# A graph network kernel on one core: the memset behind each gather of source rows is dropped

## What is computed

```python
h = relu(layernorm(x))
# layer 1: attention over the edges, 4 heads of 16
ZU = einsum('nd,kdr->knr', h, U)
zs, zd = ZU[:, src, :], ZU[:, dst, :]
logits = (zs * zd).sum(-1) / 4
alpha = softmax of logits over the edges of one dst
agg = segment_sum(alpha[..., None] * zs, dst)
x = x + relu(gradient step of h and agg with U, Dmat)
h = relu(layernorm(x))
# layer 2: message passing and a GRU cell
red = segment_sum(h[src] + relvectors[edge_type], dst)
x = x + gru(red, h)
```

## Time and profile before

| | us |
|---|---|
| median of 3 runs | 1061.5 (1060.14 to 1062.06) |
| span of the profiled execution | 1059.6 |
| gathers of source rows, first to last start | 46.87 to 722.93 |
| first and last weighing (L1083) start | 121.0 and 733.6 |
| second layer, about | 747 to 1059 |

### The profile page before, as it was taken

How to read it: one execution, slowest core, us unless ns; L and a number is a source line. 1 busy time by engine, 2 the same in 40 slices (tenths; PEclk the granted TensorE clock), 3 DMA queues, 4 the chain that set the end, 5 groups by cost and what they waited for, 6 DMA issues and landing times.

```text
span 1059.6 us, 14242 instructions
## 1 busy us (share of the span) xinstructions
PE 862.7 (81%) x4828; PEld 640.4 (60%) x4828; DVE 631.8 (60%) x1285; ACT 421.5 (40%) x804; POOL 647.8 (61%) x969
## 2 busy tenths in 40 slices
PE   6943688787788878787887786676999999999996
PEld 6741676565566656565665564464676676677773
DVE  5340577787888867777777764453243343388853
ACT  5423216555555555555565543341211111124441
POOL 4698888888888888888888888883001001000000
PEclk9996557787777777777787787787999999999998
DMA  9361334445455544554454553323344434421111
GB/s 196 77 156 36 74 78 120 119 119 125 116 128 130 132 123 112 129 123 125 119 129 111 120 124 89 88 51 84 95 126 141 124 116 137 124 87 49 50 51 34
DMA packets 54646, 112.99 MB, mean 107 GB/s; under 512 B 15435, under 2 KB 32968, under 8 KB 51443
## 3 DMA queue, kind: packets, MB, share of 16 engines
q1 hardware_dynamic: 34632, 81.38, 24.1%
q0 software_dynamic: 18880, 30.57, 17.5%
q10 hardware_dynamic: 1056, 0.07, 0.1%
HBM read 80.99 MB, written 30.86 MB: 106 GB/s over the span
## 4 chain that ended last, share of the span: by engine, by line
POOL 57%; PE 31%; issue 7%; DVE 2%; DMA 1%; SPq 1%; ACT 1%; POOLq 0%; DVEq 0%; ACTq 0%
POOL shared L724 28%; POOL cnt_rows L729 15%; POOL zs_third L724 13%; PE bank L1948 13%; PE bank L1947 6%; PE bank L1974 5%; PE bank L1975 2%; PE bank L1925 1%; PE bank L1875 1%; PE bank L1707 1%; PE bank L1971 1%; PE bank L1966 1%; DMA xs<-in_x 0%; DVE bst L885 0%; SPq L471 0%
## 5 line engine op out<-in xcount | busy, mean ns | idle before, releaser
L724 POOL DMA_INDIRECT shared<-zu_table,src_col x306 | 300.0, 980 | 51.6 <-issue 48.7
L729 POOL MEMSET cnt_rows<- 54x300 f32 x450 | 165.5, 368 | 0.3
L724 POOL DMA_INDIRECT zs_third<-zu_table,src_col x144 | 140.8, 978 | 23.0 <-issue 23.0
L999 DVE TENSOR_TENSOR setup<-iota_b,bank 128x500 bf16<-128x500 bf16 (+1 forms) x252 | 140.0, 609 | 1.1 <-PE bank L1911 0.5
L1570 ACT ACTIVATE setup<-bank 125x500 bf16<-125x500 f32 (+1 forms) x126 | 81.2, 681 | 106.5 <-PE bank L1911 70.7
L1804 PEld LDWEIGHTS bank<-zus,shared 125*128 125x128 f32 x900 | 114.0, 209 | 15.5 <-issue 14.9
L1804 PE MATMUL bank<-zus,shared 125*128 125x64 f32 x900 | 115.6, 292 | 7.8 <-ACT shared L1515 5.9
L1829 PE MATMUL bank<-layer,oh 128*125 128x84 f32 x900 | 110.1, 284 | 0.0
L1829 PEld LDWEIGHTS bank<-layer,oh 128*125 128x125 f32 x900 | 107.7, 200 | 0.1
L1911 PE MATMUL bank<-setup 128*125 128x125 bf16 x450 | 58.3, 279 | 52.0 <-DVE setup L999 42.9
L1911 PEld LDWEIGHTS bank<-setup 128*125 128x125 bf16 x450 | 48.4, 184 | 78.2 <-DVE setup L999 70.7
(11 more groups left out here) (235 smaller groups left out, 1775.8 us busy)
## 6 DMA issues: line engine op xcount, KB each, us to landing
shared<-in_edges SPq DMA_DIRECT2D x25, 1125.0 KB
counts_table<-setup SPq DMA_DIRECT2D x18, 683.6 KB
own_table<-own_out SPq DMA_DIRECT2D x25, 375.0 KB
shared<-own_table SPq DMA_DIRECT2D x25, 375.0 KB
zus<-counts_table POOLq DMA_DIRECT2D x9, 683.6 KB, 5.2
shared<-counts_table POOLq DMA_DIRECT2D x9, 683.6 KB, 5.0
shared<-zu_table,src_col POOLq DMA_INDIRECT x306
h_table<-h2s SPq DMA_DIRECT2D x25, 125.0 KB
```

The source lines that it names most:

```text
L724: nc.gpsimd.indirect_dma_start(out=zs[t % 3][:, j * KR:(j + 1) * KR], out_offset=None, in_=zu_table, in_offset=bass.IndirectOffsetOnAxis(a ...
L729: nc.gpsimd.memset(idle, 0.0).then_inc(idle_set, 1)
L999: nc.vector.tensor_tensor(chunk[n % 2][:, 0:(b - a) * W].rearrange("p (g w) -> p g w", w=W), io, ps(3, 128, at + a, at + b).unsqueeze(2).b ...
```

## The change

The memset and the wait ahead of it are taken out of the loop over columns, and with them the region, the semaphore and its first increment. Nothing else is touched.

```diff
-        idle = cnt_rows[0:3 * C, N - 300:N]
...
-        idle_set = sem("idle_set")
...
                             in_offset=bass.IndirectOffsetOnAxis(ap=src_col[:, t, j:j + 1], axis=0),
                         ).then_inc(g_zs[t % 3][c], 16)
-                        pool.wait_ge(idle_set, t * C + j + 1)
-                        nc.gpsimd.memset(idle, 0.0).then_inc(idle_set, 1)
 
             def windowed():
-                pool.sem_inc(idle_set, 1)
                 pool.wait_ge(st_zu, 16 * 2 * 5)
                 each_window(source_rows)
```

## The result

The median is 1387.6 us (4 runs, 1379.5 to 1389.4) against 1061.5 us for the kernel before in the same comparison. The ratio is 1.305, with a 95% interval of 1.301 to 1.309. The kernel became 30% slower. The forecast, 1075.5 us with a range of 1014 to 1084, was far off in size, and its mechanism isn't what happened.

A forecast was written before the change was run, and what follows sets the result against it. GpSimd's gather stream was taken to bound the first layer. The profiled span of 1059.6 us, plus 450 x (1.509 - 1.478) = 14 us for a later last gather, plus 1.9 carried over, gave 1075.5 us; range 1014 to 1084.

The forecast's parts named there:

- What bounds the kernel: First layer: its end hangs on GpSimd's last gather; GpSimd's chain ends last for 57% of the span.
- The distance between gathers: GpSimd, first layer: start of one gather to the next, predicted to go from 1.478 to 1.509 us.
- the second way: GpSimd's gather distance taken from setup gathers without a memset, record 1.20 plus gap 0.30: 1.509 us, 0.031 longer.
- the first way: GpSimd's gather distance as today's 0.953 us record plus the setup's 0.30 gap: 1.257 us, 0.221 less than now.
- what would make me wrong: Closing caveat: that the extra 0.25 us in the fifteen setup gathers' records come from their extra descriptors.
- packets are 2.5 times as many and the record is only a quarter longer: Setup gathers against the loop's: reason given for doubting that extra descriptors make their records longer.
- The whole shift lands: First layer: all 14 us by which the last gather starts later reach the end, since VectorE waits for gathers.
- rival *Faster: First layer: the memset is 0.22 us of pure delay per gather; end 46 us sooner, around 1015.5 us; chance 31%.
- rival *No change: GpSimd: memset lies wholly beside something done anyway between gathers; distance stays 1.478 us, time 1061.5 us; chance 13%.
- The worth of a shorter distance: Gather stream: each 0.01 us below a distance of 1.478 gives 4.5 us, up to a distance of about 1.38.

The follow-up runs named there:

- e15: Kernel before with the memset behind each gather 1x300 instead of 54x300: 1044.6 us, ratio 0.985.
- e18: Kernel before with the memset behind each gather 1x150 instead of 54x300: 995.5 us, ratio 0.939.
- e1: Kernel before with the memset behind each gather 1x1 instead of 54x300, wait and increment kept: 1400.7 us, ratio 1.319.
- e4: Kernel before with the 54x300 memset and its wait only behind each sixth gather: 1381.3 us, ratio 1.301.
- e11: Kernel before with a second memset of 54x30, with its own wait, added behind the 54x300 one: 1138.4 us, ratio 1.072.
- e9: Kernel before without the memset, each gather waiting until the one before it has landed: 1847.0 us, ratio 1.739.
- e5: Kernel before with the memset behind each gather 54x150 instead of 54x300: 1261.3 us, ratio 1.188.
- e12: Kernel before with the memset 54x150 instead of 54x300 from window 20 on only: 1107.7 us, ratio 1.043.
- e6: Kernel before with the memset behind each gather 54x230 instead of 54x300: 1140.4 us, ratio 1.066 from its two shortest runs.
- e13: Changed kernel with each gather fetching rows for 64 partitions instead of 128, buffers cleared once ahead: 992.2 us, ratio 0.935 against before.
- e14: Changed kernel with each gathered row 16 floats instead of 64, buffers cleared once ahead: 993.3 us, ratio 0.937 against before.
- e8: Kernel before with twelve 1x1 memsets behind each gather in place of the 54x300 one: 1089.8 us, ratio 1.025.

## Why the prediction was wrong

**What bounds the kernel** was read rightly. The first layer hung on the gather stream, and e15 to e18, each against before on its own chip, return nearly what the last gather gains: 16.7 us sooner gave 15.3 us (e15), 67.8 gave 64.8 (e18). The second layer kept its length: from the last weighing to the end 325.1 us, and 326.0 before.

**The distance between gathers** was the first wrong step. I chose the second way, 1.509 us, from the fifteen gathers of the setup, and the first way gave the right number: 0.953 + 0.30 = 1.257, measured 1.249. The reason stood in the text as what would make me wrong. In the changed kernel, with nothing behind any gather, both kinds stand side by side on GpSimd's timeline:

```profile
40.87 1.20 POOL L803 DMA_INDIRECT oh<-in_edges,src_at  x1 [0.30 <-issue]
...
47.86 0.95 POOL L722 DMA_INDIRECT shared<-zu_table,src_col  x1 [0.30 <-issue]
```

A record of 1.20 goes with the gathers that make 80 packets instead of 32, not with the absence of a memset. I had weighed "packets are 2.5 times as many and the record is only a quarter longer" against it, as if a record had to grow in proportion. By the right distance I would have forecast 1015.5 us, and missed by more.

**"The whole shift lands", and the like step of the rival *Faster*,** was the step that failed in size. Both assume that the stream acts on the other engines through one thing, the time at which rows land. The runs show a second effect, which no term of the sum held: TensorE's signals come late while gathers follow closely, 13 to 18 us in most windows and 320 us in all on L1136. On the first chip it is there at a distance of 1.249 us (e1 to e4), and gone at 1.642 (e11) and 2.702 (e9). The rival's description of GpSimd came true in every point (0.94, 0.30, waits for the weighing from the fourth window on) and the end came 326 us later instead of 46 sooner. The sign of the forecast was right by accident.

Could the profile of before have shown it? Only faintly. VectorE's wait on that line had 8.3 us in 7 pieces from "remote", longest 1.9, with the sum on TensorE long done. I read no meaning into it. It was the one wait of VectorE in the first layer, beside 3.7 us on L1064 and 0.5 us on L999, that the profile put down to no engine and no DMA. ScalarE had 16 us of it in 17 pieces.

**The rival *No change*** fell with the distance. Its idea of a memset that lies beside something the engine does anyway holds for a small one: 1x1 costs no distance (e1). The one of 54x300 costs 1.478 - 1.249 = 0.229 us.

**The worth of a shorter distance,** 4.5 us for each 0.01, "up to a distance of about 1.38": measured, where nothing is held, 15.3 us for 0.031, 36.4 for 0.090 and 64.8 for 0.157, that is 4.9, 4.0 and 4.1. The limit at 1.38 was too early. I had counted only the waits behind 555 us as VectorE's reserve.

## What to carry to other kernels

An idle instruction between DMAs can be a brake that the rest of the kernel needs: before it is removed, look for waits from "remote", or on work that has long ended, on engines that need nothing of that stream. Where a gather stream binds, its pace is a number to be tuned like a tile size: here times from 995 to 1401 us came from nothing but the size of a memset that nobody reads. Tune it on one chip, and bring the kernel that started the question along to each new one. The two groups of chips here disagree on whether a distance of 1.32 to 1.35 us helps: e18 gained 65 us on one and e5 lost 200 on the other, though their memsets differ too, one partition against 54. A count of busy times doesn't show such a loss, and neither do the gathers' own rows.

## What the runs showed of the hardware

- **Signals of TensorE come late beside a dense gather stream, in the first comparison and on the first two chips.** In the changed kernel, with gathers of 128 rows of 256 bytes 1.249 us apart, VectorE and ScalarE went on 16.3 and 18.9 us after the modelled end of TensorE's work, when the burst was over. VectorE's signal to TensorE took 0.05 us in the same burst. Where TensorE has more to do, it crawls as well, one matmul in 1.40 or 2.8 us (e12). Steps under it are multiples of 0.70 us, in the changed kernel and in e12. On the first chip a distance of 1.642 or 2.702 us holds nothing (e11, e9). On the third and fourth nothing was held in any run, down to 1.321 us with whole gathers (e18).
- The Trainium skill, SBUF — State Buffer, SBUF: two separate sides, says that engine ports and DMA ports can't contend, and that an apparent slowdown is a locked port or a gather starved of descriptors. The trace agrees in that no engine's busy time grew, and the gathers weren't starved, at a steady 1.249 us. TensorE's signals came late all the same. No run shows that SBUF has a part in that.
- **A gather has landed at most 2.7 us after its start** when none is ahead of it, since the chain of e9 steps by 2.70 us, where its record is 0.95. The Trainium skill, Perfetto Trace Analysis, DMA Instruction — SWDGE (GPSIMD), says that such a record ends when the last descriptor is written and not when the data have moved; the trace agrees.
- **The granted clock of TensorE follows the waits.** Between 200 and 880 us it is 0.66 of the full clock with held signals, against 0.77 before (200 to 555 us), and 0.99 in the second layer of both. Such a mean lies between the two levels, 1.2 and 2.4 GHz. The row of the kernel after for that stretch (behind the engines the clock, then the DMA share and GB/s):

```profile
200.00:880.00 680.00, 341.32 (x2002) 251.65 (x2001) 324.10 (x666) 233.18 (x428) 279.36 (x295) 0.66 0.32 77
```

  TensorE worked half of this stretch (341 of 680 us), and 314 of 320 us in the second layer. The clock isn't the cause of the loss, since its busy time is the same in sum.

**Left open.** Why signals are held in the runs on two chips and in none on the other two isn't shown. One rival bears on all of it: the recording. Every time in this document, before and after, is of an execution that was recorded, with its span and clock. Every trace with held signals misses increments, and with whole gathers on these chips more are missing the closer the gathers follow. Of the 7200 increments of the gathers' landings (450 x 16) the changed kernel's trace holds 1350, that of e5 1660, of e6 2418, of before 3838, of e11 5893 and of e9 all 7200; those of e13 to e18 hold 7135 or more. So the writing of these records may itself hold TensorE back, and the loss of 326 us may be smaller or absent in an execution that isn't recorded. None was timed. The changed kernel on the third or fourth chip, and e14 and e18 on the first, would tell chip, bytes and partitions apart. Nor is it shown what repeats every 0.70 us, or why twelve small memsets at 1.494 us hold 74 us (e8). With one partition and whole gathers no kernel was run between 1.321 and 1.249 us, so 995.5 us need not be the best even there.
